# A pass in another order on four engines: scores together, values together, and whole units of expert weights

## The reference

```
qkv = x @ W_attn + b_attn                    # 16 heads of 16
scores = q @ k.T / 4, masked to j <= i and j >= i - 64
att = softmax(scores) @ v
x = layernorm(x + att @ W_proj + b_proj)
expert = argmax(softmax(x @ Wr.T))           # one of 8 for each token
inter = gelu(x @ W1[expert] + b1[expert])    # 256 -> 1024, exact gelu
y = layernorm(inter @ Wo + bo + x) * gamma + beta
out = layernorm(x + y)
```

## Time and profile before

| | |
|---|---|
| median of 3 runs | 603.95 us (597.06 to 605.3) |
| the profiled execution's own time | 604.48 us |
| its span | 602.7 us |
| PE busy | 523.9 us, 87% |
| PE weight loads | 448.9 us, 74% |
| DVE busy | 430.3 us, 71% |
| ACT busy | 363.4 us, 60% |
| POOL busy | 324.0 us, 54% |
| mean granted clock of PE | 0.939 |
| HBM | 43.63 MB read, 23.62 MB written |

### The profile page before, as it was taken

One profiled execution on the slowest core, in us unless ns is written; L12 is line 12 of the kernel. 1 busy time (PEld: TensorE's weight loads), 2 busy tenths in 40 slices (PEclk: granted clock), 3 DMA queues, 4 the chain that ended last, 5 costly groups with the idle time before them and its releaser, 6 DMA issues. The chain is left out here.

```text
span 602.7 us, 29617 instructions
## 1 busy us (share of the span) xinstructions
PE 523.9 (87%) x11019; PEld 448.9 (74%) x11019; DVE 430.3 (71%) x1137; ACT 363.4 (60%) x831; POOL 324.0 (54%) x579
## 2 busy tenths in 40 slices
PE   3779797999899999998889735999999999999990
PEld 2657676777777777777767524999999999998880
DVE  4447676788887777877776556678888888886543
ACT  2436654777667667676674622776766766675450
POOL 7821333344544444434444351488888878886433
PEclk9869987999999999999998865999999999999997
DMA  9695978566677777677664002223322222221100
GB/s 198 163 226 152 242 219 200 145 185 189 178 186 200 173 198 191 176 192 172 183 170 120 28 27 62 60 86 98 101 80 73 73 82 72 72 75 48 33 9 7
DMA packets 94908, 77.46 MB, mean 129 GB/s; under 512 B 37030, under 2 KB 88367, under 8 KB 94770
## 3 DMA queue, kind: packets, MB, share of 16 engines
q1 hardware_dynamic: 91410, 67.12, 43.3%
q0 software_dynamic: 3264, 8.41, 4.0%
q10 hardware_dynamic: 96, 0.04, 0.0%
HBM read 43.63 MB, written 23.62 MB: 112 GB/s over the span
## 5 line engine op out<-in xcount | busy, mean ns | idle before, releaser
L1410 PE MATMUL ps<-v_even,w_hi 128*128 128x128 f16 (+1 forms) x1280 | 171.1, 216 | 1.6 <-DVE qs L1103 0.7
L1410 PE MATMUL ps<-v_even,w_lo 128*128 128x128 f16 (+1 forms) x640 | 132.9, 215 | 0.1
L843 ACT ACTIVATE probs<-ps,b1T 128x128 f32<-128x128 f32 (+1 forms) x320 | 87.3, 361 | 72.4 <-PE ps L1410 60.6
L1392 PE MATMUL ps<-wo_hi,ks 128*128 128x256 f16 x576 | 128.6, 273 | 1.0 <-DVE ks L1096 1.0
L1410 PEld LDWEIGHTS ps<-v_even,w_hi 128*128 x1280 | 121.5, 99 | 6.3 <-issue 3.1
L889 DVE TENSOR_REDUCE mx<-ps 128x4 bf16<-128x512 f32 x128 | 84.9, 686 | 21.8 <-PE ps L1193 21.6
L1392 PE MATMUL ps<-wo_lo,ks 128*128 128x256 f16 x288 | 78.5, 273 | 0.0
L740 ACT ACTIVATE probs<-ps 128x512 f32<-128x512 f32 x128 | 70.1, 619 | 9.1 <-PE ps L1215 8.0
L1239 PE MATMUL ps<-probs,sel 128*32 128x64 f32 x2048 | 67.8, 227 | 2.4 <-issue 2.4
L1096 DVE TENSOR_TENSOR ks<-probs,ks 128x512 f16<-128x512 f32 x72 | 55.2, 767 | 19.8 <-ACT ks L850 19.4
L1410 PEld LDWEIGHTS ps<-v_even,w_lo 128*128 x640 | 63.1, 99 | 5.6 <-issue 0.3
(11 more groups left out here) (230 smaller groups left out, 1357.4 us busy)
## 6 DMA issues: line engine op xcount, KB each, us to landing
qk_s<-qk_hi SPq DMA_DIRECT2D x64, 128.0 KB
w_in<-in_L_ffn_W_dram SPq DMA_DIRECT2D x32, 256.0 KB, 4.4
v_odd<-slots SPq DMA_DIRECT2D x64, 128.0 KB, 2.1
qs<-qk_s SPq DMA_DIRECT2D x16, 384.0 KB, 4.3
ks<-qk_s SPq DMA_DIRECT2D x16, 384.0 KB, 5.0
v_even<-v_odd SPq DMA_DIRECT2D x63, 96.0 KB, 3.7
ks<-qk_s SPq DMA_DIRECT2D x32, 144.0 KB, 4.0
qk_s<-qk_lo SPq DMA_DIRECT2D x32, 128.0 KB
```

The costliest lines, as they stand in the source:

```text
L843: last = nc.scalar.activation(g[1 - p][:, ic, n * width:(n + 1) * width], ps_h[1 - p][:, half, col + n * width:col + (n + 1) * width], ACT ...
L1392: ins = mm(ps_y[p], h[p][hs][:, ic, :], wo[ws][:, ic, :], start=n == 0, stop=n == 3 * IC - 1)
L1410: up_ins = mm(ps_h[1 - p][:, half, col + m * width:col + (m + 1) * width], weights(ws, owners[m], k, ic), sT[1 - p][ss][:, k, at], start=k ...
```

## The change

On all four engines the order inside a pass is changed.

- PE: the first scores, then the projection of tile `old`, then the other three scores, the input transposes, and all four steps of `values` in one run. The transposes of the maxima stand ahead of the values product. The ranks stand ahead of all four transposed scores.
- PSUM: the last transposed scores go to bank 7 in place of bank 4, and wait for the `rdenT` copy in place of the first exponential.
- ACT: the maxima's rows stand ahead of the copy of the values, and all four exponentials behind the copies of the reciprocals and of the queries and keys.
- DVE: all four maxima stand first. The reciprocals follow on the router's logits, then the router's choice, then the statistics, then the values' router part, then the expert and output weights, and then `att`, with the ranks' places behind it.
- POOL: the scale and shift of tile `old` stand behind the two parts of `att`.
- Expert weights: one whole unit (1024 columns) in each even pass on ACT and DVE in place of a half (512) in each pass; its load, in one DMA, is issued in the odd pass ahead. The pieces of the output weights come in passes 8, 10, 12 and 14.

The diff, cut to its core:

```diff
         ps_s = [ps[:, k, :] for k in (2, 5, 2, 3)]
-        ps_t = [ps[:, k, :] for k in (4, 5, 3, 4)]
+        ps_t = [ps[:, k, :] for k in (4, 5, 3, 7)]
...
         def wo_piece(it):
-            n = it - WO_AT
+            n = (it - WO_AT) // 2 if it % 2 == 0 else -1
...
@@ sync @@
-                n = it + 1
-                if a_tile(n):
-                    cols = slice(n % 2 * I // 2, (n % 2 + 1) * I // 2)
-                    wait(sp, w1l_done, n - 1)
-                    sp.dma_start(w1_in[:, cols], w1_units[n // 2][:, cols]).then_inc(w1_ld[n % 2], 16)
+                if it % 2 == 1 and a_tile(it + 1):
+                    n = (it + 1) // 2
+                    wait(sp, w1l_done, n)
+                    sp.dma_start(w1_in[:, :], w1_units[n]).then_inc(w1_ld[n % 2], 16)
@@ gpsimd @@
-                n = it - 2
-                if a_tile(n):
-                    pool.wait_ge(mv_done, n + 1)
...
-                    nc.gpsimd.tensor_tensor(shift_by[:, :], less_mean[:, :], rstd[:, :], ALU.mult)\
-                        .then_inc(shift_done, 1)
                 n = it - 1
...
                     nc.gpsimd.tensor_tensor(attT[1][:, :, :], att[:, :, :], attT[0][:, :, :], ALU.subtract)\
                         .then_inc(al_done, 1)
+                n = it - 2
+                if a_tile(n):
+                    pool.wait_ge(mv_done, n + 1)
...
+                    nc.gpsimd.tensor_tensor(shift_by[:, :], less_mean[:, :], rstd[:, :], ALU.mult)\
+                        .then_inc(shift_done, 1)
@@ scalar @@
-                n = it - 1
-                if a_tile(n):
-                    piece, cols = n // 2, slice(n % 2 * I // 2, (n % 2 + 1) * I // 2)
+                if it % 2 == 0 and a_tile(it):
+                    n = it // 2
                     act.wait_ge(w1_ld[n % 2], 16 * (n // 2 + 1))
-                    nc.scalar.activation(w1s[0][:, piece, cols], w1_in[:, cols], ACT.Copy, scale=W_UP)\
-                        .then_inc(w1h_done, 1)
+                    nc.scalar.activation(w1s[0][:, n, :], w1_in[:, :], ACT.Copy, scale=W_UP).then_inc(w1h_done, 1)
...
+                cur = a_tile(it)
+                if cur:
+                    act.wait_ge(mxT_done, it + 1)
+                    maxima_rows(0)
+                    maxima_rows(1)
                 if a_tile(it + 1):
                     m = it + 1
                     act.wait_ge(v_done, m + 1)
...
-                cur = a_tile(it)
-                if cur:
-                    act.wait_ge(mxT_done, it + 1)
-                    maxima_rows(0)
-                    maxima_rows(1)
-                    exps(0)
                 n = it - 1
                 if a_tile(n):
                     act.wait_ge(rdenT_done, n + 1)
...
                         .then_inc(qkh_done, 1)
+                if cur:
+                    exps(0)
@@ vector @@
-                maxima(0)
-                maxima(1)
+                for step in range(UNITS_T):
+                    maxima(step)
...
-                maxima(2)
-                maxima(3)
                 if a_tile(done):
                     dve.wait_ge(pv_done, 4 * done + 4)
...
+                if a_tile(old):
+                    dve.wait_ge(y_done, old + 1)
+                    nc.vector.bn_stats(stats[:, :], y[old % 2][:, :]).then_inc(bn_done, 1)
...
+                if a_tile(it + 1) and it + 1 > 0:
+                    router_x(it + 1)
+                if it % 2 == 0 and a_tile(it):
+                    n = it // 2
+                    dve.wait_ge(w1h_done, n + 1)
+                    nc.vector.scalar_tensor_tensor(w1s[1][:, n, :], w1_in[:, :], W_UP, w1s[0][:, n, :],
+                                                   ALU.mult, ALU.subtract).then_inc(w1l_done, 1)
+                if wo_piece(it):
+                    dve.wait_ge(whi_done, 5 + (it - WO_AT) // 2)
+                    nc.vector.scalar_tensor_tensor(wo[1][:, wo_piece(it), :], wo_in[:, wo_piece(it), :], W_UP,
+                                                   wo[0][:, wo_piece(it), :], ALU.mult, ALU.subtract).then_inc(wlo_done, 1)
                 if a_tile(done):
-                    piece, cols = done // 2, slice(done % 2 * I // 2, (done % 2 + 1) * I // 2)
-                    dve.wait_ge(w1h_done, done + 1)
...
+                    dve.wait_ge(rdenT_out, done + 1)
+                    wait(dve, al_done, done)
+                    nc.vector.tensor_tensor(att[:, :, :], ps_num, rdenT[:, :, :], ALU.mult).then_inc(att_done, 1)
                 if a_tile(old) and old % 2 == 1:
                     dve.wait_ge(rank_done, pair + 1)
...
-                if a_tile(done):
-                    dve.wait_ge(rdenT_out, done + 1)
-                    wait(dve, al_done, done)
-                    nc.vector.tensor_tensor(att[:, :, :], ps_num, rdenT[:, :, :], ALU.mult).then_inc(att_done, 1)
...
@@ tensor @@
-                    if step in (0, 3):
-                        wait(pe, exp_done, 4 * it + step // 3)
+                    if step == 0:
+                        wait(pe, exp_done, 4 * (it - 1) + 1)
+                    if step == 3:
+                        wait(pe, rdenT_out, done + 1)
...
                 scores(0)
-                values(0)
-                values(1)
-                scores(1)
+                if a_tile(old):
+                    pe.wait_ge(al_done, old + 1)
...
+                            [(wp[0][:, c, :], wp[1][:, c, :]) for c in range(CC)]).then_inc(proj_done, 1)
+                for step in range(1, UNITS_T):
+                    scores(step)
                 for t in turned(it):
...
-                scores(2)
-                scores(3)
-                values(2)
-                values(3)
+                for step in range(UNITS_T):
+                    values(step)
+                if a_tile(it):
+                    pe.wait_ge(mx_done, 4 * it + 4)
+                    for m in range(CC):
+                        last = nc.tensor.transpose(ps_mx[:, :, m, :], mx[it % 2][:, :], ident_b[:, :])
+                    last.then_inc(mxT_done, 1)
                 if a_tile(it + 1):
                     m = it + 1
...
                 if a_tile(done):
                     pe.wait_ge(rdenp_done, done + 1)
+                    pe.wait_ge(exp_done, 4 * done + 4)
...
-                scores_t(0)
-                scores_t(1)
                 if a_tile(old) and old % 2 == 1:
                     pe.wait_ge(onehot_done, old // 2 + 1)
...
+                scores_t(0)
+                scores_t(1)
                 scores_t(2)
                 scores_t(3)
...
-            pe.wait_ge(w1l_done, TILES)
+            pe.wait_ge(w1l_done, UNITS)
```

More of the change, by code:

```diff
@@ L683, in _ @@
                         .then_inc(al_done, 1)
+                n = it - 2
+                if a_tile(n):
+                    pool.wait_ge(mv_done, n + 1)
+                    wait(pool, x1_done, n)
+                    nc.gpsimd.tensor_tensor(less_mean[:, :], zero[:, :], meanvar[:, 0:1], ALU.subtract)
+                    nc.gpsimd.tensor_tensor(veps[:, :], meanvar[:, 1:2], eps_outer[:, :], ALU.add)\
+                        .then_inc(veps_done, 1)
+                    pool.wait_ge(veps_done, n + 1)
+                    nc.gpsimd.tensor_tensor(rstd[:, :], veps[:, :], power[:, :], ALU.pow).then_inc(rstd_done, 1)
+                    pool.wait_ge(rstd_done, n + 1)
+                    nc.gpsimd.tensor_tensor(shift_by[:, :], less_mean[:, :], rstd[:, :], ALU.mult)\
+                        .then_inc(shift_done, 1)
             pool.wait_ge(ffn_w_ld, 16 * FFN_LOADS)
@@ L939, in _ @@
                                                    ALU.mult, ALU.add).then_inc(rdenp_done, 1)
-                if a_tile(it + 1) and it + 1 > 0:
-                    router_x(it + 1)
                 pair = old // 2
@@ L1244, in _ @@
                 scores(0)
-                values(0)
-                values(1)
-                scores(1)
+                if a_tile(old):
+                    pe.wait_ge(al_done, old + 1)
+                    wait(pe, v_out, upto(it))
+                    wait(pe, lx_done, upto(it))
+                    wait(pe, place_done, old // 2)
+                    if old == 0:
+                        pe.wait_ge(wlo_done, 4)
+                    product(ps_proj, [tuple(attT[s][:, 2 * c:2 * c + 2, :].rearrange("p b q -> p (b q)") for s in range(2))
+                                      for c in range(CC)],
+                            [(wp[0][:, c, :], wp[1][:, c, :]) for c in range(CC)]).then_inc(proj_done, 1)
+                for step in range(1, UNITS_T):
+                    scores(step)
                 for t in turned(it):
@@ L1257, in _ @@
                     last.then_inc(xT_done, 1)
-                if a_tile(old):
-                    pe.wait_ge(al_done, old + 1)
-                    wait(pe, v_out, upto(it))
-                    wait(pe, lx_done, upto(it))
-                    wait(pe, place_done, old // 2)
-                    if old == 0:
-                        pe.wait_ge(wlo_done, 4)
```

(14 more changed lines are left out.)

24 lines of the change are left out of this document (4 added, 20 removed).

## The result

The changed kernel took 620.41 us in the median of 6 runs (614.82 to 622.72), the kernel before 602.95 in the median of 6: ratio **1.032, 95% interval 1.027 to 1.037**. The profiled execution of after took 617.25 us (span 615.5), that of before 604.48 (602.7): 12.8 us more; the medians lie 17.5 apart. Forecast were 610 us; 620 lay inside the range, but by a mechanism that was not in it, so that the range held it by luck.

The account below looks back on a forecast made before the run. The limit was to pass from PE (8.35 us of a 9.05 us pass) to a ring through DVE, ACT, POOL and PE. +4.2 - 9.3 + 5 - 1.9 + 5 + 4 - 1.5 = +5.5 on 604.48 gave 610 us, range 596 to 625.

Parts of the forecast that it names:

- Small gaps of PE: Ordinary passes: small PE gaps fall where PE now waits anyway, -1.5 us.
- The ring: Chain through DVE, ACT, POOL and PE limits passes: 8.8 us odd, 9.65 even, +4.2 us over 27 passes.
- Late keys: Two long passes where PE waited for DMA-late keys, nearly cured by earlier issues: -9.3 of 10.3 us.
- Output weights: Four pieces ahead of att, even passes 8 to 14: +5 us, old cost -1.9, clock loss +5.
- Last passes: From tile 28, no query and key product fills PE and the clock falls: 0.8 us more for five passes, +4.
- the third: Rival: keys still come late, since 512 KB and 1 MB loads share engines; cure 0, 619 us; chance 0.1.
- The clock in ordinary even passes: Rival: 1.4 us idle ahead of the projection drops PE's clock in 10 of 13 even passes, +17, 627 us; chance 0.25.

Follow-up runs that it names:

- experiment 1: Changed kernel with weight units 1 to 15 loading 16 of 1024 columns (stale weights): 614.66 us, ratio 1.015.
- the order alone: New order on all engines, with the weights by halves in every pass as in the kernel before: 611.54 us, ratio 1.011.
- experiment 6: Kernel before with the four value blocks in one run behind the fourth scores, in place of two and two: 642.43 us, ratio 1.054.
- experiment 9: Changed kernel with value blocks 0 and 1 ahead of the projection, y and logits ahead of the third maxima on DVE: 610.26 us, ratio 1.000.
- experiments 5: Changed kernel with the value blocks on PE cut into two and two again: 645.34 us, ratio 1.060.

## Why the prediction was wrong, point by point

All differences here are between the two profiled executions, stretch by stretch and with the gaps taken out, so that the gaps stand once, in their own term.

- **Small gaps of PE, -1.5: the step that failed.** I counted them as a leftover that hides in PE's new waits, without asking where they come from. They grew from 5.5 to 21.7 us, +16.1. The trace of before held a hint that I did not follow, its 5.5 us of such idle time; I took it for noise where it was the edge of a limit.
- **The ring** (forecast 8.8 and 9.65, mean 9.2, +4.2 us): right in form. Undisturbed passes alternate by 8.69 and 9.44, att starts 2.99 and 3.92 behind the values' end (297.21 and 305.91), the weights' low part takes 1.22. From att to the next end of values are 5.5 to 5.7, and PE waits 1.38 for POOL in one pass and not at all in the next (forecast 1.4 and 0.5). Mean 9.06, so the term is about 0. The eleven intervals from 188.87, which hold nothing else, are 1.1 longer than before, and the two ahead of the keys 0.3 shorter.
- **Late keys, -9.3**: one of two was cured. The first wait stayed (2.49 us; window 76 to 80 at a clock of 0.71); with the unit's load made tiny it is gone (experiment 1). The three passes from 73.90 take 34.9 us for 37.2 before, and 4.3 of these are gaps (0.8 before): -5.8 without them.
- **Output weights, +8.1 in all, clock included**: the clock was 1.00 from 105 to 180, so the +5 for it did not come. The eight intervals from 108.79 take 80.1 us, for 74.5 before, but 5.7 us of gaps lie there (0.7 before): +0.6. Against the order alone it is +3.0, about what I had for the pieces themselves (5 less 1.9).
- **Last passes, +4**: the clock fell (0.57 at 330) but the last five intervals are 46.3 us for 48.3 before, with gaps of 2.1 and 1.7: -2.4.
- **Not in the sum: the first passes.** The first copy comes 1.85 us later and the two first intervals take 21.5 us for 18.2, without a gap in them: +5.1. The two intervals take 20.3 us or more in the eight kernels with the new order or a variant of it and 18.8 or less in the five with the old one, and the clock stays low longer (0.50 from 40 to 45 us, 0.80 from 45 to 50, for 0.85 and 1.00 before). The first copy itself comes between 28.5 and 33.0 in all these kernels, at 32.85 in experiment 6 with the old order: that 1.85 says little.

Sum of what was measured: 16.1 + 1.1 - 0.3 - 5.8 + 0.6 - 2.4 + 5.1 = 14.4, of 14.5 found up to the last copy; the rest, behind it, is 1.7 shorter. The forecast of +5.5 came nearer than its terms deserve: the gaps were put 17.6 us too low, the keys 3.5 and the first passes 5.1, while output weights, last passes and ring were 17.3 too high. Of the rivals none was it, though one wait for keys of the third did stay. The clock in ordinary even passes held at 1.00 from 105 to 180 although PE waited there six times for POOL, 7.2 us together, 1.2 us in the mean. The Trainium skill describes a kernel whose clock swings with frequent short idles ("TensorE: Matmul & The Clock Gate", section "A second HAM failure mode: psum-queue depth-cycling"); six such idles in 75 us did not do it here. What the sum lacked was a column for instructions: how many a stretch of PE needs, and how fast they come.

What stays open: when a packet is asked for and what holds its start back (for the gap of 5.92 us in experiment 9 PE stops at 85.97 and the packet starts at 89.5), the short paired gaps of experiments 5 and 6, and why order and units together cost two points more than the order alone at the same sum of gaps.

## What to carry to other kernels

Count TensorE's instructions, not only its busy time: each matmul of the trace comes with a weight load, and a float32 matmul of the code is two of them. See how many pass between two packets of the instruction queue. Where small matmuls use 256 up in 2 us, keep other work between them (experiment 6 shows what joining them cost), and do not count on a denser order or a shorter wait elsewhere as long as a packet takes 3.5 to 6 us. A row "issue" in the table of waits of an engine that should be full deserves a look before the change, since it is the one row that a plan made of semaphores cannot price.

## What the runs showed of the hardware that I had not expected

- TensorE ran dry in a straight line of code: 128 matmuls with their loads, then 1.1 to 2.0 us of nothing with quiet DMA engines, 2.6 to 3.8 beside the 8 MB of loads.
- In the passes too every such gap of the kernels before and after ends 2.3 to 3.3 us behind the start of a 16 KB packet of the instruction queue.
- Such a gap can cost twice: behind 3.77 us of it the next 128 matmuls took 3.64 us in place of 1.99.
- POOL's cast of 256 columns took 1.32 us in place of 0.40 while DVE read two operands from SBUF, and 0.40 beside qk_lo, whose one operand comes from PSUM.
- Four float32 matmuls of 32 weight columns in four strips overlap: groups of eight start 0.11 us apart, and the one of 256 columns that replaces four made the run of values 1.2 us longer.
